# Decoder layer with an RWKV-6 recurrence: the second level's acceptance reads its tokens in runs of two, and the split of g's input moves up in two queues

## The reference

```python
xx  = shift(x) - x;  xxx = x + xx * maa_x
a   = tanh(xxx @ w1)                        # five groups of 32
m   = a[f] @ w2[f]                          # f = w, k, v, r, g
xf  = x + xx * (maa_f + m_f)                # five mixed inputs
r, k, v = xr @ Wr.T, xk @ Wk.T, xv @ Wv.T;  g = silu(xg @ Wg.T)
w   = decay + tanh(xw @ wd1) @ wd2          # decay of each token and channel
# for each head of 64 channels, token by token:
y_t = r_t . (S + u * k_t v_t^T);  S = exp(-exp(w_t)) * S + k_t v_t^T
out = (groupnorm(y) * g) @ Wo.T
```

## Time and profile before

| | |
|---|---|
| median of 3 runs | 938.38 us (935.85 to 938.78) |
| the profiled execution | 946.25 us, of which the profile's span is 944.4 us |
| TensorE busy (matmuls) | 837.3 us, 89% of the span |
| VectorE busy | 760.6 us, 81% |
| ScalarE busy | 502.4 us, 53% |
| GpSimd busy | 126.6 us, 13% |
| recurrence and its projections | about the first 540 us of the span |
| one full step in the middle (steps 4 to 7) | 53.6 us |

### The profile page before, as it was taken

The page is one execution under the profiler, slowest core; times in us unless marked ns, Lnnn a source line. Parts: engine busy times, 40 slices in busy tenths (PEclk is TensorE's granted clock), DMA queues, the critical chain, the costliest instruction groups (busy, mean ns, idle before and its releaser), DMA issues.

```text
span 944.4 us, 23407 instructions
## 1 busy us (share of the span) xinstructions
PE 837.3 (89%) x9913; PEld 676.8 (72%) x9930; DVE 760.6 (81%) x1213; ACT 502.4 (53%) x719; POOL 126.6 (13%) x202
## 2 busy tenths in 40 slices
PE   2377699999999999898989899999999977989995
PEld 1276688888888988887878688888888734545552
DVE  4868797979798897987476487789888988989983
ACT  3464365463736456361533354445453365979994
POOL 3000001020101002010100100000000124343431
PEclk9588799999999999999788999999999988999999
DMA  9511101112030200115050222330332322132220
GB/s 221 142 47 56 57 14 62 42 46 69 12 102 14 91 25 36 46 42 185 2 175 6 70 85 93 135 121 28 118 133 90 103 68 68 68 123 79 90 79 33
DMA packets 36968, 72.65 MB, mean 77 GB/s; under 512 B 6466, under 2 KB 7234, under 8 KB 35850
## 3 DMA queue, kind: packets, MB, share of 16 engines
q1 hardware_dynamic: 35754, 68.20, 21.4%
q0 software_dynamic: 1120, 3.10, 1.5%
HBM read 57.66 MB, written 12.58 MB: 74 GB/s over the span
## 4 chain that ended last, share of the span: by engine, by line
PE 51%; DVE 28%; issue 9%; ACT 4%; POOL 4%; DMA 3%; SPq 1%; DVEq 0%; ACTq 0%; POOLq 0%
PE P L62 7%; PE P L64 6%; PE P L63 6%; PE S L2193 5%; PE P L2183 4%; PE S L710 4%; POOL sm L376 3%; DVE rec L1784 2%; DVE E L1778 2%; PE P L638 2%; DVE K L1001 2%; DVE xf L953 2%; DVE R L998 2%; PE S L667 1%; PE P L785 1%
## 5 line engine op out<-in xcount | busy, mean ns | idle before, releaser
L376 POOL TENSOR_TENSOR sm<-sm,mhalf 128x16 f32<-128x16 f32 x8 | 30.6, 3826 | 341.3 <-DVE sm L1050 341.3
L710 PE MATMUL S<-R,K 64*64 64x32 f32 x3072 | 62.5, 229 | 13.9 <-DVE K L1001 7.4
L710 PEld LDWEIGHTS S<-R,K 64*64 64x64 f32 x3072 | 56.1, 144 | 22.3 <-issue 12.3
L2183 PE MATMUL P<-wq,xqT 128*128 128x512 bf16 x240 | 65.0, 392 | 2.5 <-ACT xqT L2112 1.2
L2193 PE MATMUL S<-wq,hqT 128*128 128x512 bf16 x255 | 62.8, 393 | 5.0 <-ACT hqT L2126 5.0
L953 DVE TENSOR_TENSOR xf<-P,xx 128x1024 f32<-128x1024 f32 x40 | 48.9, 1222 | 12.0 <-PE P L638 11.8
L1778 DVE TENSOR_SCALAR E<-S,upper 128x2048 f32<-128x2048 f32 x16 | 37.6, 2350 | 24.3 <-PE S L1626 24.1
L1784 DVE RECIPROCAL rec<-S 128x512 f32<-128x512 f32 x16 | 53.6, 3351 | 3.1 <-PE S L1641 3.0
L1452 ACT ACTIVATE E<-E 128x2048 f32<-128x2048 f32 x16 | 30.6, 1913 | 43.9 <-DVE E L1778 43.8
L998 DVE TENSOR_TENSOR R<-R,D 128x256 f32<-128x256 f32 x96 | 41.7, 434 | 12.4 <-PE S L710 11.9
L960 DVE TENSOR_TENSOR xf<-xf,xnT 128x1024 f32<-128x1024 f32 x40 | 49.0, 1226 | 0.8
(11 more groups left out here) (288 smaller groups left out, 2730.7 us busy)
## 6 DMA issues: line engine op xcount, KB each, us to landing
wch<-in_wff SPq DMA_DIRECT2D x32, 256.0 KB, 3.2
cwch<-in_wff SPq DMA_DIRECT2D x8, 1024.0 KB, 6.7
xt<-in_x SPq DMA_DIRECT2D x8, 512.0 KB, 4.8
y<-in_x SPq DMA_DIRECT2D x8, 512.0 KB, 3.5
out<-y SPq DMA_DIRECT2D x8, 512.0 KB, 3.3
cxt<-out SPq DMA_DIRECT2D x8, 512.0 KB, 4.2
ct<-in_ctx SPq DMA_DIRECT2D x8, 512.0 KB, 5.3
cxr<-out SPq DMA_DIRECT2D x8, 512.0 KB, 6.8
```

The source lines that it names most:

```text
L376: pool.tensor_tensor(sm[:, 2, :], sm[:, 1, :], mhalf[:, 0:2 * H], ALU.pow).then_inc(y_rstd, 1)
L710: mm = pe.matmul(ps[half_rows(side), par, b, k, :], K[head_rows(par), r % 2, at:at + HALF], right_tokens(par, g, side, i), start=True, sto ...
L2183: pe.matmul(Hp[:, cols], xqT[t % 2][:, k, :], w1q[:, k, cols], start=k == 0, stop=False)
```

## The change

1. `accept`: the `rearrange` for level 1 is gone; its two tokens are the innermost loop, as at the other levels.
2. ScalarE: `hi(p, 3)` stands ahead of `abs_sum(p, 2)`, and so ahead of `split_weight("o")` (step 2) and of the norm activations.
3. VectorE: `lo(p, 3)` stands ahead of `mix(p, 4)`.

```diff
@@ scalar, step @@
             if f:
+                hi(p, 3)
                 abs_sum(p, 2)
             if q == 0:
                 split_weight("o")
...
             if f:
-                hi(p, 3)
                 abs_sum(p, 3)
@@ vector, accept @@
             mask = wide(masks[:, i, :].rearrange("p (n m) -> p n m", m=m).unsqueeze(1), [P, 4 * NC, HALF // 2 // m, m])
-            if i == 1:
-                out, got, mask = (t.rearrange("p g n m -> p g m n") for t in (out, got, mask))
             dve.copy_predicated(out, mask, got).then_inc(A_part, 1)
@@ vector, step @@
             if f:
+                lo(p, 3)
                 mix(p, 4)
-                lo(p, 3)
                 xf_sum(p, 4)
```

## The result

The kernel after took 929.05 us (median of 4 runs, 926.39 to 930.80) against 938.58 us (4 runs, 935.85 to 940.33); the ratio is 0.990, 95% interval 0.986 to 0.994. Measured again twice, with 12 runs each, the same kernel gave 0.995 (0.992 to 0.998) and 0.996 (0.994 to 0.998). Over all runs in this study the medians are 937.4 us before (89 runs) and 932.7 after (28 runs): 4.7 us.

What follows compares the result with a forecast made beforehand. The prediction took TensorE to bound full steps, VectorE and ScalarE the first steps. It summed -6.9 (full steps), -0.4 (step 10) and +2.8 (opening) to -4.5 us: 933.9 us from 938.38, range 930 to 937 (8 in 10).

Steps and rivals of the forecast that it cites:

- The part 1 copy at 0.70 us: Level 1's predicated copy on VectorE would take 0.70 us in runs of two, bounds 0.70 and 2.48 us.
- a copy over 1 us: Sign that would show the prediction wrong: level 1's predicated copy taking over 1 us instead of near 0.7.
- Parts 2 and 3 in full steps: VectorE's 1.4 us wait for ScalarE's high half of g goes; norm activations not later, 1.3 us of cover before TensorE's transposes.
- Gain: 7.4 - 0.5 (step 10) = 6.9 us in steps 3 to 8: TensorE's waits for VectorE's update of K at levels 1 and 3 all go in these steps, winning 6.9 us.
- The bound of 2.4 us a step: TensorE is busy 51.2 us of a full step's 53.6, so at most some 2.4 us of each can be won.
- 52.2 to 52.4 us: Expected length of a full step after the change, instead of 53.6 us.
- In full steps part 1 is worth only some 0.1 us more: Parts 2 and 3 alone would nearly remove the full steps' waits; the faster level 1 copy adds some 0.1 us.
- The opening's 2.84 us: Cost in steps 1 and 2 of making g's halves earlier: 0.76 + 0.95 + 1.13 us, bounds 0.8 and 2.84.
- Step 1's 0.76: In step 1 the low half goes ahead of the mix, so TensorE's transposes start 0.76 us later.
- Step 10's 0.4 us: TensorE's wait in step 10 for the cross attention's x goes, winning 0.4 us; bounds 0.4 and 1.7.
- rival A: Larger gain: TensorE works on after its issue stalls in the last steps and the 2.38 us stall shrinks; 930.2 us, chance 0.13.
- rivals B and C: B: level 1's wait returns, 936.3 us, chance 0.2; C: copy in runs of two slower, 949 us, chance 0.06.

Runs made afterwards that it cites:

- e5: Kernel after with level 1's copy in eight access patterns, one per pair: 0.71 to 0.74 us contiguous destination, 1.30 or 1.31 runs of two, 2.45 single words.
- e6: Kernel after with level 1's acceptance replaced by a small memset; one execution, profiled span 934.2 us, steps 3 to 8 259.1 us.
- e1: Kernel before with only the rearrange of level 1's copy taken out (part 1 alone): ratio 0.996 (0.993 to 0.999).
- e2: Kernel after with level 1's rearrange put back (parts 2 and 3 alone): ratio 0.999 (0.996 to 1.002) to the kernel before.
- e4: Kernel after, but g's halves keep their old places in both queues for pairs 0 and 1: ratio 0.993 (0.990 to 0.996) to the kernel before.

## Why the prediction was right or wrong, by its steps

- **The part 1 copy at 0.70 us: wrong,** by the prediction's own sign, a copy over 1 us. It takes 1.31 us, of which 1.10 of the queue; e5 shows why. I had taken R's update in the same runs (0.42 us) as the nearest row. A plain product doesn't pay for a broken destination, a predicated copy does. The bounds held. It cost the sum next to nothing, since in full steps the copy is covered (e6).
- **Parts 2 and 3 in full steps: right.** The wait for xgh is gone, the norm activations aren't later, TensorE's transposes aren't held.
- **The failed step: "Gain: 7.4 - 0.5 (step 10) = 6.9 us in steps 3 to 8", that is 1.3 to 1.4 per step, 6.7 in steps 4 to 8.** Measured: 9.0 us over these five steps, 1.8 each. The missing 0.4 per step are the second halves' waits inside the bursts of 1.34 us, which count as busy (e1): the mechanism was right, and its term was too small. A step without a stall takes 51.7 us and has won 1.9 to 2.0: 1.3 to 1.4 as booked, 0.4 inside the bursts, and up to 0.2 that I haven't traced. The bound of 2.4 us a step was not passed, but it was taken from a busy time that held 0.4 of waiting. The forecast's 52.2 to 52.4 us are met by luck, in steps 5 and 7 alone, where a stall of TensorE's own issue gives some of it back.
- **"In full steps part 1 is worth only some 0.1 us more": wrong.** B is 263.0 without it and 259.8 with it, 0.6 a step. Seen in the trace are the waits of 0.3 to 0.5 us that e2 still has at level 3 in three of the five steps, with the same hidden part inside their bursts.
- **The opening's 2.84 us: right in its parts** (0.81, 0.89 and 2.07 for the last two together, and 2.1 back in e4). Step 1's 0.76 is seen in the idle time alone, not in the length of the opening. A grew by less than 2.1, on average by 1.1 (57.3 to 58.4, single profiles 0.4 to 2.2), for it also holds step 3's own levels, and they gained about 1: A is 57.3 before and 56.3 with the opening spared, where I had booked 0.2.
- **Step 10's 0.4 us: the wait went, its worth is open.** TensorE's wait for `cxl` is 0.34 to 0.37 us in all three profiles of the kernel before and 0.8 in e2, and gone in every kernel with part 1, as in these rows of the kernel after:

```profile
483.08 0.44 PE L710 MATMUL S<-R,K 64*64 64x32 f32 x9 [2.40 <-issue]
483.46 0.58 PE L62 MATMUL P<-cxl,Xqh 128*128 128x256 f32 x1
```

  What that gave the whole can't be told, since C scatters by 4 us. The stall ahead of it is there in all profiles (1.9 to 2.9 us), which speaks for the lower bound.
- **The sum and rival A.** The stages give -9.0 (B), about + 1.1 (A) and + 0.8 (step 1, by its idle time): some -7 us. The first measurement gave -9.5, the pooled medians -4.7 (95%: 2.2 to 6.2 us less). Rival A's extra gain, that TensorE's stalls shrink, isn't it: in step 9 the longest is 2.9 us in all three profiles of before and 3.2 to 4.1 in those of after, in step 10 2.4 against 1.9 to 2.4. So the 5 us between the 9.5 measured and the 4.5 forecast have two parts. Some 2.6 us are in the stages: 2.3 in B, the waits sized too small, and 0.7 in A, less the 0.4 of step 10 that can't be read. The other 2.4 no stage shows; they are in the first four runs alone, and their cause is open (the runs of the kernel after spread from 926.4 to 937.1). Why the pooled medians show 2 to 3 us less than the stages is not settled either. The two lengths of the ffn are one candidate, if the kernel after falls into the longer more often than the one before, but one long profile of three for each can't show it. The prediction's rivals B and C fell: level 1's wait didn't come back, and the copy got faster. Its own range was not worked out to its end either: with -1.3 and -2.0 the lower end of the forecast would have been 930.6, not 931.5.

## What to carry to other kernels

An instruction burst that lasts longer behind a wait holds more waits inside; compare its duration with the like burst that didn't wait before pricing the gain. When an order is better in the steady steps, look at the first ones by themselves: here the opening paid 2.9 us of idle time, and a condition on the step gives it back. And where executions scatter by 1%, the stretch between two instructions of the touched stage, repeatable here to 0.2 to 0.7 us, says more than a handful of whole times.

## What the runs showed of the hardware that I had not expected

- A predicated copy of 128x512 from PSUM costs by the breaks of its destination: 0.71 us contiguous or in runs of four, 1.31 in runs of two, 2.45 in single words, while neither the source in PSUM nor the mask matters in steps of two or in runs of two stepping four. A product (TENSOR_TENSOR) in the same runs takes 0.42 us for 256 elements like a contiguous one. By the rule of the Trainium skill cited in the prediction (Vector Engine (DVE) Microarchitecture Reference, the section on the SBUF access granule), runs of two run at full rate from an even word and not from an odd one. Here the measurement differs: the copy took 1.31 us on both, where a contiguous one took 0.71.
- The same program's ffn takes 148.1 to 148.6 us or 151.4 to 151.8 for the same work; the longer profiles have one more stretch of half clock, 3.4 us long.
- TensorE's longest stalls of its own issue stay in steps 9 (2.6 to 4.1 us) and 10 (1.9 to 2.9) in all profiles, and some show only once a wait ahead of them is gone: in step 5 (0.2 to 0.6 us) and mostly in step 7 (0.2 to 0.3).
